# Retuning the order tables of a Mamba and mixture-of-experts kernel

## The reference

```python
h = _layernorm(x, ln_g, ln_b)
xz = h @ W_in;  x_in, z = jnp.split(xz, 2, axis=-1)          # 256 -> 2 x 512
x_c = silu(_causal_depthwise_conv(x_in, conv_w, conv_b))     # 4 taps
dt, Bm, Cm = jnp.split(x_c @ W_xproj, [64, 80], axis=-1)
delta = softplus(dt @ W_dt + b_dt);  A = -exp(A_log)         # 16 states
# for every token t:  s = exp(delta*A)*s + delta*B*u;  y = sum_n s*C
y = (y + u * D) * silu(z)
x1 = x + ln(x) + y @ W_out
# experts: logits = ln(x1) @ Wg + bg; top 2, softmax over the two
# out = x1 + LN(ln(x1) + sum_k w_k * (relu(ln(x1) @ W1_e + b1_e) @ W2_e + b2_e))
```

## Time and profile before

| what | value |
|---|---|
| median of three runs | 2457.19 us |
| the profiled execution's own time | 2457.69 us |
| its span, first to last instruction | 2455.9 us |
| around the span | 1.8 us |
| mean granted TensorE clock | 0.96 |
| busy: PE, DVE, POOL, ACT | 89%, 83%, 75%, 62% |
| PE's weight loads | 72% |
| first scan of the first chunk, end of the last scan | 44.1 us, 1827.6 us |
| a chunk, start to start, chunks 1 to 13 | 111.0 to 112.5 us |

### The profile page before, as it was taken

How to read it: one execution, slowest core, us unless ns; L and a number is a source line. 1 busy time by engine, 2 the same in 40 slices (tenths; PEclk the granted TensorE clock), 3 DMA queues, 4 the chain that set the end, 5 groups by cost and what they waited for, 6 DMA issues and landing times. The chain is left out here.

```text
span 2455.9 us, 47537 instructions
## 1 busy us (share of the span) xinstructions
PE 2187.4 (89%) x13697; PEld 1771.4 (72%) x13698; DVE 2047.4 (83%) x3052; ACT 1512.3 (62%) x3337; POOL 1830.4 (75%) x1107
## 2 busy tenths in 40 slices
PE   7889899998989899998989898999777999999980
PEld 4667677677767676766767676676676999999970
DVE  5899999999998999999999999999983555555558
ACT  6677777778787877777787868787741111111107
POOL 3888989889898988898898989889962444444447
PEclk9999999999999999999999999999987999999995
DMA  5041423314040413223140414233236999989978
GB/s 170 6 134 51 132 74 100 109 65 155 28 156 33 141 59 124 91 82 132 46 158 21 155 49 133 68 107 102 73 109 187 230 227 229 227 230 228 230 161 274
DMA packets 186504, 312.25 MB, mean 127 GB/s; under 512 B 18819, under 2 KB 117795, under 8 KB 186212
## 3 DMA queue, kind: packets, MB, share of 16 engines
q1 hardware_dynamic: 140164, 256.94, 33.5%
q0 software_dynamic: 25584, 34.62, 7.4%
q10 hardware_dynamic: 20592, 18.65, 2.3%
HBM read 247.09 MB, written 63.06 MB: 126 GB/s over the span
## 5 line engine op out<-in xcount | busy, mean ns | idle before, releaser
L819 POOL TENSOR_TENSOR dbu<-du,bb 128x1024 f32<-128x1024 f32 x384 | 904.9, 2365 | 105.7 <-DVE ps_a L633 77.4
L1121 ACT ACTIVATE ps_a<-dl,a_neg 128x512 f32<-128x512 f32 x768 | 518.4, 685 | 196.2 <-DVE ss L633 183.5
L836 POOL TENSOR_TENSOR wp<-ss,rows_c 128x1024 f32<-128x1024 f32 x192 | 453.1, 2360 | 38.5 <-DVE ss L633 38.2
L1718 POOL DMA_INDIRECT acc_scratch<-ow,idx x135 | 211.1, 1564 | 314.3 <-issue 122.4
L645 DVE TENSOR_TENSOR wd<-ps_a,rows_c 128x1024 f32<-128x1024 f32 x320 | 383.0, 1197 | 0.0
L1393 PEld LDWEIGHTS ps_y<-ident,wd 128*128 128x128 f32 x2560 | 300.6, 143 | 87.9 <-issue 73.5
L1393 PE MATMUL ps_y<-ident,wd 128*128 128x128 f32 x2560 | 339.9, 277 | 11.3 <-DVE wd L645 11.3
L1420 PEld LDWEIGHTS ps_a<-dg,duT 128*128 128x128 f32 x2048 | 254.8, 199 | 64.3 <-issue 62.9
L1758 ACT COPY e_meta<-xt 128x2 f32<-128x2 f32 x135 | 26.0, 192 | 442.1 <-PE e_ps_x L1828 442.1
L1420 PE MATMUL ps_a<-dg,duT 128*128 128x128 f32 x2048 | 264.2, 283 | 29.7 <-ACT carry L1128 27.0
L1646 DVE TENSOR_SCALAR e_hT<-e_ps_h,b_turned 128x128 f32<-128x128 f32 x540 | 152.0, 344 | 148.8 <-PE e_ps_h L1837 141.2
(11 more groups left out here) (199 smaller groups left out, 3674.4 us busy)
## 6 DMA issues: line engine op xcount, KB each, us to landing
w<-in_L_ffn_W_dram SPq DMA_DIRECT2D x135, 512.0 KB, 4.7
rows_c<-b_scratch SPq DMA_DIRECT2D x128, 512.0 KB, 5.3
bb<-b_scratch SPq DMA_DIRECT2D x96, 512.0 KB, 4.4
xt<-xs_scratch SPq DMA_DIRECT2D x135, 129.0 KB, 4.0
xb<-in_L_attn_x_dram SPq DMA_DIRECT2D x16, 512.0 KB, 4.0
hx<-in_L_attn_x_dram SPq DMA_DIRECT2D x16, 512.0 KB, 6.2
x_scratch<-hx SPq DMA_DIRECT2D x16, 512.0 KB, 2.9
acc_scratch<-stage SPq DMA_DIRECT2D x16, 512.0 KB, 2.9
```

Source lines behind the costliest of these rows:

```text
L819: pool.tensor_tensor(dbu[:, k % NBU], du[:, g % 2, :].unsqueeze(1).broadcast_to([P, 2, CH]), bb[:, row:row + 2, :], ALU.mult).then_inc(dbu ...
L836: pool.tensor_tensor(wp[:, s % 2], ss[:, s % 2], cc[:, rows, :], ALU.mult).then_inc(wp_done, 1)
L1121: act.activation(dst, dl[:, g, :], ACT.Exp, scale=a_neg[:, g, n:n + 1]).then_inc(exp_done, 1)
L1718: pool.indirect_dma_start(out=acc_dram, out_offset=bass.IndirectOffsetOnAxis(ap=idx[:, old, :], axis=0), in_=ow[:, old, :], in_offset=None ...
```

## The change

The change writes other numbers into the tables that set the order. Each instruction stays what it was, and all of them are still there; the SyncE queue and its DMAs are the same. Two of the lines, with the halo's:

```diff
-                  ("out", 1, -1, 17, 2, 5), ("conv", 0, 1, 20, 1, 3), ("x", 2, 1, 20, 2, 3), ("x", 3, 1, 21, 2, 4),
+                  ("out", 1, -1, 17, 2, 5), ("x", 2, 1, 20, 2, 3), ("conv", 0, 1, 21, 1, 3), ("x", 3, 1, 21, 2, 5),
-        HALO_AT = 3
+        HALO_AT = 0
-        NORM = (55, 59)
+        NORM = (57, 61)
-        FACTOR_X1 = 17
+        FACTOR_X1 = 16
-        DRIVE = (4, 5, 10, 10)
+        DRIVE = (4, 4, 10, 10)
-        WEIGH_P = {4: 0, 8: 1, 10: 2}
+        WEIGH_P = {4: 0, 7: 1, 10: 2}
```

More of the change, by code:

```diff
@@ L265, in mamba_block @@
         STEADY = [("h", 0, 1, 0, 1, 3), ("h", 1, 1, 0, 1, 5), ("back", 3, -1, 6, 1, 3), ("x", 0, 1, 7, 2, 3),
-                  ("dt", 2, 0, 8, 1, 2), ("out", 0, -1, 11, 2, 3), ("turnu", 1, 0, 12, 1, 4), ("x", 1, 1, 14, 1, 8),
-                  ("out", 1, -1, 17, 2, 5), ("conv", 0, 1, 20, 1, 3), ("x", 2, 1, 20, 2, 3), ("x", 3, 1, 21, 2, 4),
+                  ("dt", 2, 0, 8, 1, 2), ("out", 0, -1, 11, 2, 3), ("turnu", 1, 0, 12, 1, 3), ("x", 1, 1, 14, 1, 8),
+                  ("out", 1, -1, 17, 2, 5), ("x", 2, 1, 20, 2, 3), ("conv", 0, 1, 21, 1, 3), ("x", 3, 1, 21, 2, 5),
                   ("conv", 1, 1, 23, 4, 6), ("dt", 3, 0, 27, 1, 2), ("conv", 2, 1, 27, 3, 5),
-                  ("turnu", 2, 0, 34, 1, 2), ("conv", 3, 1, 32, 4, 6), ("turnx", 0, -1, 37, 1, 4),
+                  ("turnu", 2, 0, 35, 1, 2), ("conv", 3, 1, 32, 4, 6), ("turnx", 0, -1, 37, 1, 4),
                   ("turnx", 1, -1, 37, 1, 4), ("logit", 0, -1, 40, 1, 4), ("dbc", 0, 1, 41, 1, 2),
                   ("bturn", 0, 1, 42, 1, 4), ("back", 1, 0, 42, 1, 4), ("back", 0, 0, 43, 1, 4),
-                  ("rank", 0, -1, 43, 1, 0), ("turnu", 3, 0, 47, 1, 2), ("dt", 0, 1, 49, 1, 0),
-                  ("dt", 1, 1, 49, 1, 2), ("z", 0, 1, 54, 2, 2), ("z", 1, 1, 56, 1, 1), ("z", 2, 1, 57, 2, 6),
-                  ("turnu", 0, 1, 60, 1, 2), ("back", 2, 0, 62, 1, 4), ("z", 3, 1, 61, 2, 4)]
-        HALO_AT = 3
+                  ("rank", 0, -1, 43, 1, 0), ("turnu", 3, 0, 47, 1, 2), ("dt", 0, 1, 48, 1, 1),
+                  ("dt", 1, 1, 49, 1, 3), ("z", 0, 1, 54, 2, 3), ("z", 1, 1, 56, 1, 2), ("z", 2, 1, 57, 2, 6),
+                  ("turnu", 0, 1, 60, 1, 2), ("back", 2, 0, 62, 1, 4), ("z", 3, 1, 61, 2, 5)]
+        HALO_AT = 0
         XL_AT = 11
@@ L278, in mamba_block @@
         SILU_Z = 73
-        NORM = (55, 59)
-        ADD_DT = ((49, 0), (51, 1), (74, 2), (95, 3))
+        NORM = (57, 61)
+        ADD_DT = ((50, 0), (51, 1), (74, 2), (95, 3))
         RESIDUAL = ((5, 0), (5, 1))
         STATS = (47, 49)
-        INV_STD = (52, 53, 57)
+        INV_STD = (52, 54, 55)
         FACTOR = 29
-        STATS_X1 = (24, 24)
-        INV_STD_X1 = (25, 28)
-        FACTOR_X1 = 17
[L288 to L293, removed]
+        STATS_X1 = (25, 26)
+        INV_STD_X1 = (28, 32)
+        FACTOR_X1 = 16
+        XN = (33, 38)
+        ROUTE = (38, 39, 40, 40, 40, 41, 41, 41, 41, 41, 45, 46, 46, 46)
+        EXP_W = (43, 46, 46)
+        IDS_0 = 46
+        IDS_1 = 58
+        SCATTER = ((25, 0, 0), (25, 0, 1), (26, 0, 2), (29, 0, 3), (30, 1, 0), (31, 1, 1), (34, 1, 2), (36, 1, 3))
         DIAGONALS = (54, 57, 62, 62)
-        DRIVE = (4, 5, 10, 10)
+        DRIVE = (4, 4, 10, 10)
         KEEP_EARLY = (4, 9)
@@ L299, in mamba_block @@
         TURN_P = {9: 0, 15: 1, 20: 2}
[L300 to L301 removed]
+        SKIP_Y = 8
+        WEIGH_P = {4: 0, 7: 1, 10: 2}
         DU_AT = 6
```

## The result

The changed kernel takes 2480.61 us (median of 4 runs, 2480.20 to 2481.95), beside 2455.15 (four runs) for the kernel before. The ratio is 1.0104, interval 1.0087 to 1.0122: slower, by some 25 us. Against the kernel before as it ran beside the experiments (medians of 17 to 35 runs, 2451.4 to 2452.7) it is 28 to 29 us, and all 29 runs of the changed kernel on record have a median of 2480.6 (2473.0 to 2487.5). The prediction was 2446, range 2437 to 2460, and had given slower 0.12. The prediction was wrong.

The account below looks back on a forecast made before the run. PE's stream was taken to bound each chunk from the gate to about step 29, DVE from there to the next gate; -4.5 - 1.2 - 3.3 - 0.9 + 1.1 - 3.0 = -11.8 us from 2457.69 gave 2446, range 2437 to 2460.

Parts of the forecast that it names:

- Step 57: The scan's 0.3 to 0.7 us wait for its decay in ten of sixteen chunks goes: gain 4.5 us, ends 0 and 5.
- What could become late: POOL's two thin places: FACTOR_X1 at steps 32 and 33, 1.0 us in hand; even chunks' last weighing behind scatters moved ahead.
- the sum: All costed terms added: -11.8 us against the profiled execution's 2457.69 us, giving 2446.
- Rival 1: DVE's small waits come back, filled by others of ACT, or clock stretches take the gain: 2451 to 2460 us; chance 0.31.
- Rival 3: POOL becomes late, PE waits for the weighed states at step 36, slower than before: 2467 us; chance 0.11.
- Step 21: The scan's wait for PE, 35 us over chunks 0 to 14, goes but is given back at step 26: gain 0.
- The rule of the Trainium skill: Weight-load share, not matmul busy time, shows TensorE's headroom; by it PE had a quarter left and 35 us would be won.
- step 3: The scan's 0.22 us loss behind a late decay goes as ACT's halo and "z" 3 move: gain 3.3 us, ends 0 and 3.5.
- POOL stands idle ahead of L785: POOL waits 4.5 us for ACT's inv_std of step 32, with 1.0 us still in hand before PE wants the weighing.
- the routing one step later: POOL's first scatter waits 1.2 us longer, felt only in chunk 15: cost 1.1 us, ends 0 and 2.5.
- Behind the logits the half-clock stretch: The 1.2 GHz stretch makes step 42's scan wait in ten chunks; two fewer saves 3.0 us, ends +6 and -10.

Follow-up runs that it names:

- b_pe: Kernel before with PE's part of the change alone (DRIVE, x 2 ahead of conv 0, x 3 emptied a step later): 2451.52 us, ratio 0.9995.
- b_act59: Kernel before with ACT's part alone (halo, lags of "z", INV_STD), second half of the LayerNorm left at step 59: 2446.63 us, ratio 0.9984.
- a_norm59_x1: The change with row data at 60, second-half scatters, LayerNorm at 59, x1 statistics, FACTOR_X1 and WEIGH_P all back, against the kernel before: 2446.08 us, ratio 0.9985.
- a_sc27: The change with the fourth scatter of the first half two pairs of steps earlier in POOL's loop: 2453.65 us, ratio 1.0015 to the kernel before.

## Why the prediction was wrong, step by step

**The step that failed** is a half sentence in "Step 57": "The decay of step 58 gets 'z' 1 and the 1.0 us of row data in front, and lands about when DVE asks." I counted the moved piece by its busy time. I did not count the wait at its head, for a landing, which cost nothing at step 60 because ACT came late enough. Before, ACT reached L982 8.0 us after the fourth scatter's issue in chunk 8 and the landing took 7.1 (below): 0.9 us in hand. Over chunks 1 to 13 it was 0 to 2.4 us, and in chunks 14 and 15 ACT already waited, 0.8 and 1.5 us. The change brought ACT there 3.3 us after the issue (1052.32 - 3.31 - 1045.73). The two steps of `IDS_1` alone made 14.6 us of loss in the old kernel; in the change ACT came another 1.3 us sooner and the scatter was issued 0.9 us later. Taken away by the earlier scatter, the wait gave back 27.0 us. The rows to see it stood in the trace of before.

A second step failed beside it, in "What could become late": the scatters that move ahead of step 0 stood in the sum with nothing, covered by "some 1.2 us more before DVE notices". In chunks 2 to 14 of the change PE waits 1.1 to 1.4 us at step 3 and 0.5 to 0.7 at step 8 for POOL, which had these scatters in front, and moving them back gave 9.4 us.

**Which rival was it?** None as written. Rival 1 named waits of DVE for ACT between steps 54 and 62, the decay of step 58 "on the edge", and was right on the place; it had them fill 10 us of gains, not cost 27. Rival 3, POOL late, came true in part: PE did wait for `wp`, not at step 36 but at steps 3 and 8, through the early scatters and not through `FACTOR_X1`. The 15 us of its sum, for a wait at step 36, did not come.

**The ledger**, by medians: 2480.61 - 26.96 (fourth scatter earlier) - 9.39 (second half back) - 3.00 (routing back) = 2441.26. What is left of the change gains 10.2 us on before; the sum, without its 1.1 for the routing, had 12.9. How the 10.2 fall to its terms was not measured one by one. The sum also started from a long execution of before (2457.69, where the later medians are 2451.4 to 2452.7), so its 11.8 us would have given about 2440 there.

**Right:**
- Step 21: its wait is gone and 3.00 us stand at step 26 in even chunks, 2.3 to 2.9 in odd ones (predicted 3.5 and 2.3). b_pe shows the exchange alone. DVE in the change, chunk 8, the scan of step 26:

```profile
997.42 2.34 DVE L633 TENSOR_TENSOR_SCAN ps_a<-dbu,ps_a 128x512 f32<-128x512 f32 x2 [3.00 <-PE ps_a L1420]
```

  The rule of the Trainium skill that I weighed (Perfetto Trace Analysis, Identifying the Most-Contended Engine), by which PE had a quarter left, does not hold for this stream: the order by which it would gain 35 us gained nothing. The section names the rate of arithmetic (MFU) beside the weight loads, which I did not weigh.
- Step 57 and step 3: no wait there in the change, and none to speak of in b_act59, which gained 4 to 5 us where the two terms had 7.8.
- POOL stands idle ahead of L785, 7.20 us where I had 4.5, at no cost that a_norm59_x1 could show. ACT's part came 0.5 us later than reckoned (54.3 us into the chunk instead of 53.8), and POOL was there 2.2 us sooner (47.1 instead of 49.3):

```profile
1005.39 0.20 POOL L785 TENSOR_TENSOR x_ln<-x_ln,nm 128x4 f32<-128x4 f32 x1 [7.20 <-ACT x_ln L941]
```

**Mis-sized:** the routing one step later, 1.1 us (ends 0 and 2.5), measured 3.0; in the traces 4.6 us go in chunk 15, where I had put it, 2.9 at step 62 and 2.4 ahead of chunk 1, against 6.5 us more after the last scan. Behind the logits the half-clock stretch reached the scan of step 42 in 4 chunks of 14, not in 8, and saved 8.6 us instead of 3, but the new stretches behind PE's idle time ahead of "z" 3 came in; so the clock moved with the waits. What these new stretches cost apart from the waits that make them was not isolated.

## What to carry to other kernels

A piece that is moved takes the wait at its head along. Before moving it, read when the engine reaches it today and when what it waits for is done; the difference is all the room there is, and a wait that shows 0 in the profile may have 0.9 us left, or none. In a table of times for engines that never reorder, entries come in chains (here scatter, landing, row data, scatter), and the chain must be moved from its first link.

## What the runs showed of the hardware

**The landing of an indirect scatter goes with what else moves.** Each moves 129 KB. In chunk 8 of the kernel before, the first two took 3.5 and 2.9 us to land, and the fourth 7.1 us. The windows of before over the first two and over the fourth:

```profile
1022.90:1027.90 5.00, 4.56 (x30) 3.21 (x29) 5.00 (x8) 2.75 (x6) 4.50 (x4) 1.00 0.35 120
...
1036.40:1043.40 7.00, 7.00 (x43) 5.03 (x42) 6.67 (x7) 6.89 (x18) 6.78 (x4) 1.00 0.90 270
```

The DMA share is 0.35 in the one and 0.90 in the other, at the end of the chunk, where the 512 KB loads of the next chunk's rows of B and C run. The lines on the fourth scatter of chunk 8, of before and then of a_sc27, where it lands within a stretch (1026.7 to 1031.0) with a share of 0.39:

```profile
DMA to landing us min/median/max: 7.1/7.1/7.1
```

```profile
DMA to landing us min/median/max: 4.3/4.3/4.3
```

In chunk 15, which has no next chunk to load for, the fourth scatter of the kernel before lands after 2.6 us, at a share of 0.14. So an earlier issue pays twice here, by the time that it is earlier and by 2.8 us of landing. The Trainium skill (DMA: Bandwidth & Descriptors, Anatomy of one DMA) gives about 2.0 us plus the bytes over the full rate, 2.3 us here by estimate, which is near the 2.9 us of the quiet window and far from 7.1. The Trainium skill says in its section on queues and completion order (the same page) that each DMA engine takes turns between its queues packet by packet; the trace agrees as far as a share of 0.90 goes with the long landings, and no run here separated it.

**PE's idle time may cost again when it ends.** The gaps of about 5 us ahead of "z" 3 are followed by matmuls at a granted clock of 0.50, 2.08 us for what takes 1.02. Such a stretch of 3.4 or 6.8 us stands at steps 58 to 60 in every chunk from 1 to 14 of the change. In the kernel before none stands there; nine of its chunks have one at step 51 or 52, six of them behind one at the logits. In a_sc27, where PE idles 1.6 to 2.3 us there in chunks 1 to 13, such a stretch is left in two chunks of the 14. The stretches go with the long gaps, then, but that the idle time makes them is not shown: no run held PE busy there and left the rest alone.
